# 8x8 diagonal blocks inverted by substitution on GpSimd, one block a partition, in a gated delta-rule layer

## What is computed

```python
mixed = silu(causal_conv4(xn @ W_qkv))            # q, k, v
q = l2norm(q) * DK ** -0.5;  k = l2norm(k)
beta = sigmoid(xn @ W_b)
g = -exp(A_log) * softplus(xn @ W_a + dt_bias)     # log-decay, per token and head
def step(S, xs):                                   # over the tokens
    S = S * exp(gt)
    kS = einsum('bhk,bhkv->bhv', kt, S)
    S = S + bt * kt[:, None] * (vt - kS)[None, :]
    return S, einsum('bhk,bhkv->bhv', qt, S)
o = o * rsqrt(mean(o*o) + 1e-6) * norm_w * silu(xn @ W_z)
s = o @ W_out
return x + s * silu(ffn(xn))
```

## Time and profile before

| | us |
|---|---|
| median of 3 runs | 3300.76 |
| lowest and highest | 3298.25 and 3307.96 |
| the profiled execution | 3309.87 |
| its span | 3308.3 |
| mean granted TensorE clock of the span | 0.967 of full |
| recurrent_block's loop, first to last bq copy | 527.0 to 3217.9 |

### The profile page before, as it was taken

One profiled execution on the slowest core, in us unless ns is written; L12 is line 12 of the kernel. 1 busy time (PEld: TensorE's weight loads), 2 busy tenths in 40 slices (PEclk: granted clock), 3 DMA queues, 4 the chain that ended last, 5 costly groups with the idle time before them and its releaser, 6 DMA issues.

```text
span 3308.3 us, 126027 instructions
## 1 busy us (share of the span) xinstructions
PE 2972.5 (90%) x50836; PEld 2152.4 (65%) x50836; DVE 1875.7 (57%) x4171; ACT 1568.0 (47%) x4801; POOL 929.5 (28%) x1388
## 2 busy tenths in 40 slices
PE   2599998999999999999999999989898999999995
PEld 2255556667676766676766676767676777767664
DVE  3222226666565656666666565656565666666663
ACT  2111114555555555554555555555455555555552
POOL 0111102323332333332333232323333332333230
PEclk9799999999999999999999999999999999999997
DMA  1422200000001010100000000000000000000001
GB/s 37 136 54 54 54 11 17 18 18 14 21 11 25 11 24 11 23 11 21 15 21 14 21 15 20 14 22 14 21 15 18 16 18 18 18 18 18 18 18 54
DMA packets 207077, 80.75 MB, mean 24 GB/s; under 512 B 186368, under 2 KB 193808, under 8 KB 206352
## 3 DMA queue, kind: packets, MB, share of 16 engines
q1 hardware_dynamic: 200336, 54.60, 7.3%
q0 software_dynamic: 6144, 17.83, 2.2%
HBM read 47.63 MB, written 2.17 MB: 15 GB/s over the span
## 4 chain that ended last, share of the span: by engine, by line
PE 49%; issue 11%; DVE 9%; DMA 6%; SPq 5%; POOL 3%; ACT 1%; DVEq 0%; POOLq 0%; ACTq 0%
PE rps L772 10%; PE rps L814 6%; PE rps L824 5%; DMA bq<-bmat 4%; PE rps L693 4%; PE rps L745 4%; SPq L592 4%; DVE conv L1225 3%; PE rps L631 3%; PE rps L685 2%; PE rps L664 2%; PE rps L738 2%; PE rps L728 2%; PE rps L789 2%; PE rps L646 2%
## 5 line engine op out<-in xcount | busy, mean ns | idle before, releaser
L1225 DVE SCALAR_TENSOR_TENSOR conv<-rps,w_in,conv 128x509 f32<-128x509 f32 (+2 forms) x768 | 572.0, 745 | 107.0 <-ACT conv L1014 88.8
L772 PE MATMUL rps<-xnT,w_in 128*128 128x512 f32 x1024 | 542.6, 655 | 56.7 <-issue 56.3
L1393 POOL TENSOR_TENSOR decay_b<-decay,beta_k 128x512 f32<-128x512 f32 x128 | 130.5, 1040 | 984.3 <-DVE wsuf_b L1244 984.3
L1277 DVE TENSOR_TENSOR xq<-rps,xq 128x256 f32<-128x256 f32 x256 | 108.7, 425 | 478.4 <-PE rps L824 478.4
L1014 ACT ACTIVATE conv<-rps,w_in 128x512 f32<-128x512 f32 x256 | 176.0, 688 | 311.2 <-PE rps L772 309.6
L772 PEld LDWEIGHTS rps<-xnT,w_in 128*128 128x128 f32 x1024 | 185.5, 202 | 203.5 <-issue 194.2
L1060 ACT ACTIVATE wq<-rps 128x256 f32<-128x256 f32 x256 | 98.4, 384 | 432.0 <-PE rps L814 432.0
L814 PEld LDWEIGHTS rps<-xqT,bqs 32*32 32x32 f32 x16384 | 167.6, 105 | 162.6 <-issue 147.1
L814 PE MATMUL rps<-xqT,bqs 32*32 32x32 f32 x16384 | 200.4, 194 | 80.1 <-POOL bqs L1419 53.2
L685 PE MATMUL rps<-w_outn,gatedT 128*128 128x256 f32 x1056 | 269.7, 389 | 0.7 <-ACT gatedT L959 0.7
L693 PE MATMUL rps<-w_z,xnT 128*128 128x256 f32 x1040 | 265.5, 388 | 2.0 <-ACT z L965 2.0
(11 more groups left out here) (194 smaller groups left out, 6123.0 us busy)
## 6 DMA issues: line engine op xcount, KB each, us to landing
scale<-comb_rows POOLq DMA_DIRECT2D x40, 256.0 KB, 5.5
w_in<-in_w_in SPq DMA_DIRECT2D x17, 520.0 KB, 4.0
bq<-bmat SPq DMA_DIRECT2D x256, 32.0 KB, 1.9
inv<-xq SPq DMA_DIRECT2D x256, 32.0 KB
w_z<-in_w_z SPq DMA_DIRECT2D x17, 256.0 KB, 2.6
w_out<-in_w_out SPq DMA_DIRECT2D x17, 256.0 KB, 2.7
invT<-xqT SPq DMA_DIRECT2D x128, 32.0 KB
wd<-in_ffn_down SPq DMA_DIRECT2D x1, 2176.0 KB, 33.1
```

Of the source, the lines that this page charges most:

```text
L772: last = nc.tensor.matmul(ps[PROJ_BANK[j]][:, :], w_in[:, m * 4 * P + j * P:m * 4 * P + (j + 1) * P], xnT[:, m, b * T:(b + 1) * T], start= ...
L1225: nc.vector.scalar_tensor_tensor(conv[:, j, shift:T], ps[PROJ_BANK[j]][:, 0:T - shift], w_in[:, k:k + 1], conv[:, j, shift:T], ALU.mult, A ...
```

## The change

Two things are done in another way.

**Small blocks.** The levels 2 and 4 go, with pairs. In their place each of the 128 blocks of 8x8 (16 along the diagonal, times 8 units) is brought to a partition of its own: SP stores the 16 diagonal blocks of bmat to DRAM (b8_dram), loads them as b8 (one block per partition, 64 elements), POOL inverts all of them at once by substitution (substitute, two instructions of 64 elements and twelve of 6 to 12 elements, each waiting for the one before), SP stores the result x8 to DRAM and loads it into the 16 places of xq. first_transpose on DVE waits for these loads. The levels 8 and 16 follow as before.

**Log-decays.** prepare_block sums the log-decays with g split in two parts, stores the sums as rows in DRAM (g_rows), and a step loads both rows, broadcast to 128 partitions, 1 MB (sums_row). log_decays is now a sum of 1024 elements per partition, a select and two sums of 512 on POOL, and exp_decay is eight activations of 128x128 with a bias instead of two of 128x512. The product log_decay on PE goes, and hide_later too.

The order of the calls on PE, ACT, DVE and POOL is another one. The core of the diff:

```diff
-LEVELS = (2, 4, 8, 16)
+S8 = 8
+LEVELS = (8, 16)
@@ sync, per step @@
                     sp.dma_start(cols[(b + 1) % BATCH][:, :], prep[:, bass.ds(step, 1), :]).then_inc(cols_in, 16)
+                    at = sp.snap(step * (U * C))
+                    sp.dma_start(sums_row[:, :, :, :].rearrange("p k u t -> p k (u t)"),
+                                 g_rows[:, bass.ds(at, U * C)].unsqueeze(0).to_broadcast([P, 2, U * C])).then_inc(rows_in, 16)
...
                     after(b_done, n(2) + 2)
+                    for k, rows in enumerate(SMALL):
+                        sp.dma_start(b8_dram[k].rearrange("u r c -> r u c"), bmat[rows, :, rows]).then_inc(b8_out, 16)
                     for rows in BLOCKS:
                         sp.dma_start(bq[rows, :, :], bmat[rows, :, rows]).then_inc(diag_in, 16)
+                    after(b8_out, i * (256 * BATCH) + 256 * (b + 1))
+                    sp.dma_start(b8[:, :, :], b8_dram.rearrange("k u r c -> (k u) r c")).then_inc(b8_in, 16)
+                    after(x0_done, n(X0) + X0)
+                    sp.dma_start(x8_dram.rearrange("k u r c -> (k u) r c"), x8[:, :, :]).then_inc(x8_out, 16)
+                    after(x8_out, i * (16 * BATCH) + 16 * (b + 1))
+                    for k, rows in enumerate(SMALL):
+                        at = (k % (Q // S8)) * S8
+                        sp.dma_start(xq[rows, :, at:at + S8], x8_dram[k].rearrange("u r c -> r u c")).then_inc(xq_in, 16)
@@ tensor, end of a step @@
                     pe.wait_ge(acc_done, n(2) + 1)
                     project_z(tb, 2)
+                    merge_w(0)
+                    attend(2)
+                    merge_x(0)
+                    read_state(3)
                     merge_w(1)
                     by_token(3)
                     solve(3)
-                    merge_x(2)
+                    merge_x(1)
+                    project_z(tb, 3)
                     attend(3)
-                    pe.wait_ge(v_done, n(2) + 1)
-                    log_decay(n(1) + 2, 0)
-                    merge_w(3)
-                    pe.wait_ge(v_done, n(2) + 2)
-                    log_decay(n(1) + 2, 1)
-                    merge_x(3)
@@ scalar @@
-                nc.scalar.activation(decay[:, g * NC_:(g + 1) * NC_, :],
-                                     ps[D_BANK[g]][:, :].rearrange("p (c t) -> p c t", c=NC_), ACT.Exp).then_inc(decay_done, 1)
+                for c in range(NC_):
+                    u = g * NC_ + c
+                    last = nc.scalar.activation(decay[:, u, :], log_d[:, u, :], ACT.Exp, bias=col(k, NLO, u))
+                last.then_inc(decay_done, 1)
@@ vector @@
                     def first_transpose():
-                        dve.wait_ge(x0_done, n(2) + 2)
+                        dve.wait_ge(xq_in, i * (256 * BATCH) + 256 * (b + 1))
@@ gpsimd @@
+                nc.gpsimd.tensor_tensor(log_d[:, :, :], sums_row[:, 0, :, :],
+                                        cols[k][:, NHI * U:(NHI + 1) * U].unsqueeze(2).to_broadcast([P, U, C]), ALU.add).then_inc(g_done, 1)
...
+                nc.gpsimd.affine_select(log_d[:, :, :], log_d[:, :, :], [[0, U], [1, C]], ALU.is_ge, MASKED,
+                                        base=0, channel_multiplier=-1).then_inc(g_done, 1)
+                for g in range(REP):
+                    us = slice(g * NC_, (g + 1) * NC_)
+                    nc.gpsimd.tensor_tensor(log_d[:, us, :], log_d[:, us, :], sums_row[:, 1, us, :], ALU.add).then_inc(g_done, 1)
...
+                    def substitute():
...
+                        nc.gpsimd.memset(xq[:, :, :], 0.0).then_inc(x0_done, 1)
+                        pool.wait_ge(b8_in, i * (16 * BATCH) + 16 * (b + 1))
...
+                        for k in range(S8 - 2):
+                            s = S8 - 2 - k
+                            shape = [P, s, S8 - 1 - s]
+                            pool.wait_ge(x0_done, n(X0) + 3 + 2 * k)
+                            nc.gpsimd.tensor_tensor(t8[:, 0:s, s + 1:S8], b8[:, 0:s, s:s + 1].to_broadcast(shape),
+                                                    x8[:, s:s + 1, s + 1:S8].to_broadcast(shape), ALU.mult).then_inc(x0_done, 1)
+                            pool.wait_ge(x0_done, n(X0) + 4 + 2 * k)
+                            nc.gpsimd.tensor_tensor(x8[:, 0:s, s + 1:S8], x8[:, 0:s, s + 1:S8], t8[:, 0:s, s + 1:S8],
+                                                    ALU.subtract).then_inc(x0_done, 1)
...
                     decays_by_beta(0)
                     decays_by_beta(1)
-                    log_decays((b + 1) % BATCH, i * (16 * BATCH) + 16 * (b + 2), n(2) + 2)
-                    pairs()
+                    k_norms()
                     mask_level(0)
+                    substitute()
+                    log_decays((b + 1) % BATCH, i * (16 * BATCH) + 16 * (b + 2), n(2) + 2, n(4) + 4)
                     mask_level(1)
-                    mask_level(2)
+                    output_norms(n, 1 - p)
                     q_norms()
-                    k_norms()
-                    mask_level(3)
-                    hide_later()
-                    output_norms(n, 1 - p)
```

More of the change, by code:

```diff
@@ L313, in _ @@
             pe.wait_ge(g_ready, 1)
-            for k, at in enumerate((UPTO, AFTER, ONES)):
-                nc.tensor.matmul(ps_g[k][:, :], cst[:, at:at + P], g[:, :], start=True, stop=True).then_inc(sums_ps, 1)
+            for k, (at, src) in enumerate(((UPTO, g_hi), (UPTO, g_lo), (AFTER, g), (ONES, g))):
+                nc.tensor.matmul(ps_g[k][:, :], cst[:, at:at + P], src[:, :], start=True, stop=True).then_inc(sums_ps, 1)
+            pe.wait_ge(sums_out, 2)
+            for k, src in enumerate((sum_hi, sum_lo)):
+                for q in range(UNITS // P):
+                    last = nc.tensor.transpose(ps_t[k][:, q * P:(q + 1) * P], src[:, q * P:(q + 1) * P], ident)
+                last.then_inc(rows_ps, 1)
             pe.wait_ge(comb_ready, 1)
@@ L850, in _ @@
                     project_out(n, 0, loads)
+                    solve(1)
                     project_out(n, 1, loads)
-                    read_state(1)
-                    pe.wait_ge(qsq_done, n(1) + 1)
-                    project_out(n, 2, loads)
-                    solve(1)
+                    by_token(0)
                     k_products(0)
                     attend(1)
+                    by_token(2)
+                    read_state(2)
                     pe.wait_ge(wz_in, (i + (1 if b == 0 else 2)) * 16)
@@ L1374, in _ @@
             pool.wait_ge(init, 5)
[L1375 removed]
+            log_decays(0, 16, BASE, BASE)
             with pool.Fori(0, NK) as i:
```

267 lines of the change are left out of this document (142 added, 125 removed).

## The result

| | before | after |
|---|---|---|
| median of 4 runs of each on one chip | 3299.5 us (3296.4 to 3308.0) | 3747.6 us (3741.6 to 3751.6) |
| ratio | | 1.135, 95% interval 1.132 to 1.138 |
| span of the profiled execution | 3308.3 us | 3739.9 us |
| mean granted clock | 0.967 | 0.885 |
| period of a step | 42.7 us | 49.2 us |

The direction was right and so was the mechanism, a ring that became longer than PE's work. The time lies 422 us under the forecast of 4170 us and 32 us under the low end of 3780 us.

A forecast was written before the change was run, and what follows sets the result against it. It took a dependent ring through SP's queue and DRAM, not PE's 38.1 us, as the bound: 39.7 + 16.4 = 56.1 us per step. 3309.9 + 858 + 10, less 9, gave 4170 us; range 3780 to 4450.

The forecast's parts named there:

- the ring: Chain from one bmat through SP's queue, DRAM, substitution and merges to the next bmat; sets the period, 39.7 + 31p us.
- p: Time from one small DMA's issue to the next on SP's queue; taken as 0.53 us.
- step 1: After bmat SP issues 16 stores, then four bq copies, b8's load behind; POOL is past mask and clear at 16p + 5.3.
- Step 6: From the last transpose to the end of bmat: 14.0 us, with 12.5 and 16.3 as ends.
- Rivals A: Issues on SP's queue are small and PE stays the bound: about 3010 us, faster; chance 4%.
- C: Issues cost as the bq copies do, p = 0.65, or small blocks land late: about 4410 us; chance 16%.
- D: POOL becomes the bound; not priced, chance under 1%.
- B: Issues cost as a plain store does, p = 0.38: period 51.5 us, 3875 us in all; chance 16%.
- The size of p: Step choosing p for SP's small DMAs: between 0.38 and 0.65, 0.53 us taken from xs<-in_x, giving a 56.1 us period.
- the clock: PE cools waiting before merge_w(0), so the merges run at half clock: 3.0 us per step, between 0 and 6.
- the end of an iteration: A loop iteration's end stops PE for 3.46 us every fourth step: 0.9 us per step.
- Outside the ring: Added work in preparation and a first step that waits for longer log_decays: 10 us.

The follow-up runs named there:

- e2: The changed kernel with the first head's four gating instructions on DVE moved from ahead of the halves copy and bmat to behind bmat: 3716.4 us, ratio 1.120.
- e5: The changed kernel without POOL's log-decay work and the 1 MB broadcast, so its output lacks the decays: 3744.6 us, ratio 1.131.
- e6: The changed kernel with a padded DRAM layout: four 32x32 stores and one load out, one store and four loads back: 3270.4 us, ratio 0.989.
- e4: The changed kernel with nine extra 128x512 products on PE in its wait ahead of merge_w(0): 3680.1 us, ratio 1.111.
- e7: The kernel before with only the log-decay half of the change, the four merge levels kept: 3345.6 us, ratio 1.011.
- e8: e6 with two of the four stores and loads issued by ACT, and the first head's gating behind bmat: 3350.0 us, ratio 1.011.
- e10: e6 with two of the four stores and two of the four loads issued by ACT, gating left in place: 3170.1 us, ratio 0.961.
- e11: e6 with the log-decays formed as in the kernel before: 3392.4 us, ratio 1.028.

## Why the prediction was right about the ring and wrong about its length

**Right.** The period is set by the ring and not by PE; PE waits before merge_w(0) in every step, and DVE waits over 10 us for xq. The stages of the substitution, of the stores and loads and of the rest hold within 1.0 us up to the first transpose once p is known (table above). The queue does what step 1 said: the four copies of bq and the load of b8 stand behind sixteen stores. Step 6 was forecast at 14.0 and measured at 14.3, though partly for another reason, which is luck: the collision on DVE, which the prediction didn't have, is worth 0.8 us of it (e2). Its terms also add up to 13.2 us and not to the 13.1 given. The log-decays lie beside the ring (e5). Rivals A, C and D are out; B came nearest, with a p of 0.38.

**Wrong: the step "The size of p".** It took 0.53 between 0.38 and 0.65; p is 0.346 us. In 31 issues that is 5.7 us per step, 365 us of the 422. The choice went by the form of the access pattern: xs<-in_x was nearest because it has three dimensions and DRAM on one side. The number of dimensions did not decide it: all of these have three, and in these traces a DMA of 8 partitions x 8 units x 8 elements, 64 pieces of 32 bytes, cost 0.346, one of 32 x 8 x 32, 256 pieces of 128 bytes, 0.45 to or from DRAM (e6: four in 1.80 us) and 0.65 from SBUF to SBUF. Bytes alone don't decide it either: the store of x8, 128 pieces and 32 KB, took 0.35. That it goes by the number of pieces would fit, but no run varied that alone. The low end of the range was also drawn too tightly, at the cheapest row seen plus a gap, though the new DMAs were smaller than anything in the rows.

**Wrong in size: the clock.** 3.0 us taken, 1.3 measured (e4): 1.7 x 64 = 110 us. The half speed lasts through one merge and a few products and is over before the projection of k.

**Wrong in size: the end of an iteration.** 0.9 us per step taken, from PE's gap of 3.46 us. Steps within an iteration take 46.2 to 48.2 us, those across its end 54 to 57 (here the stores start at 2059.95 and at 2116.91); the mean, 49.2, is 2.4 us over the 46.8. The trace of before could have told most of it: its step across the end takes 48.0 us and the next one 40.1 (bq copies, the first of the three at 2020.99):

```profile
2068.98 2.61 SPq L592 DMA_DIRECT2D bq<-bmat  x4
2109.07 2.56 SPq L592 DMA_DIRECT2D bq<-bmat  x4
```

Part of the excess in the changed kernel is on ACT: two table loads of 1.28 us, once per iteration (16 of each), on the path of the projections at 2099.00 and 2103.43 us, of which the first:

```profile
2099.00 1.28 ACT L1054 ACT_TABLE_LOAD   x1 [3.33 <-PE rps L818]
```

**Outside the ring** the prediction had 10 us; the first series starts 13.2 us later than the first copies of before (540.2 and 527.0 us), 9.3 of it already in e7.

With the true p the formula gives 39.7 + 10.7 = 50.4 us, 1.2 over the mean of 49.2: clock and stages were too long by 2.7, the iteration's end too short by 1.5. Then 4170 - 365 - 64 x 1.2 = 3728; some 6 us more outside the ring, and profiled and median times that stand 15 us otherwise to each other than before (6 us under the median, not 9 over it), make 3749.

## What to carry to other kernels

When small pieces move through DRAM inside a dependent chain, count the DMA instructions on one queue, not bytes: here 31 issues of 0.35 us were 11 of 47 us, and a padded layout that lets one DMA address all blocks, with the other eight shared between two queues, turned 13.5% slower into 4% faster. Price a new kind of DMA from rows of the same size as well as the same form, and let the low end go under the cheapest row when the new one is smaller. An edit that won time on one ring can lose it on a shorter one (gating), and work that was free beside the one can cost time beside the other (the log-decays): measure the combination, not the sum.

## What the hardware showed that was not expected

- Issue times on SP's queue: 0.306 us (0.346 from one to the next) for 8 partitions x 8 units x 8 elements between SBUF and DRAM, 0.45 for 32 x 8 x 32, 0.65 for the latter from SBUF to SBUF. ACT's queue issued at about the same pace (0.81 to 0.85 us for two in e8 and e10, SP's 0.83).
- DVE's gating, two inputs in SBUF: 1.12 us for four alone, 2.77 beside POOL's decay_b, whose own instructions took 1.06 us a piece on average (1.04 before).
- PE's last product before its wait ended at 2027.9 us. The granted clock was 1.00 until 2031, 0.50 from 2032 to 2041, and 1.00 again from 2042, PE having returned at 2036.7.
- GpSimd: 0.20 to 0.21 us for 6 to 12 elements per partition, 0.32 for 64, 0.31 for a clear of 256; dependent ones 0.29 us apart.
- Every activation table load took 1.28 us, and where nothing else held the next activation it followed at once (2007.31 and 2008.60 in e11).
